# Two of sixteen state inputs made in the token layout and turned back by TensorE

## The chip, the cores and the metric

One NeuronCore of a Trainium2 chip runs the whole program in one launch. The metric is the device time of one execution in microseconds. Three runs of the kernel before gave 2841.64, 2836.22 and 2837.58 us, median 2837.58.

## What is computed

The input is 8 sequences of 1024 tokens with 256 features, all in fp32. A state space layer comes first, then a mixture of experts. Cut to what matters here:

```
xn      = layernorm(x)
u       = causal_conv4(xn @ Wx)                 # 512 channels, 4 taps
dt      = clip(sigmoid(u @ Wdt + b), 1e-4, 1)   # per token and channel
Bm, Cm  = u @ Wb, u @ Wc                        # 16 states each, per token
for each token t, channel d, state n:
    s[d,n] = exp(-dt[t,d]*A[d,n]) * s[d,n] + dt[t,d]*Bm[t,n]*u[t,d] + 1e-6
    y[t,d] = sum_n s[d,n]*Cm[t,n] + D[d]*u[t,d]
x       = x + (y * silu(z)) @ Wout
x       = x + top-2-of-8 experts(layernorm(x)) + gated shared expert(layernorm(x))
```

## The kernel before

The 8192 tokens are cut into 32 chunks of 256. Four chunks make a sequence, so the scan state is carried from the first to the second, third and fourth chunk of each sequence and starts from zero in the first. The 512 channels lie as 4 blocks (`KD`) of 128 partitions with the 256 tokens of the chunk along the free axis, so one state of one chunk is a tile of 128x1024, handled in two halves of 128x512, each in one of three PSUM banks (`V_BANKS`) that are used in turn.

`run` calls `Body.__call__` once per chunk on every engine, and each call walks 16 slots written out by hand. A call works on three chunks at once: `scan` is the chunk whose state n is scanned in slot n, `proj` is the next one (convolution, dt, B, C, z), and `post` is the one before (output projection, norm, routing, shared expert). `norm` is the one after `proj`. Each engine has its own program order, and the engines meet only at semaphores. For one state n of `scan`:

- GpSimd (POOL) multiplies `dtu` = dt*u by row n of B: `b_times_dtu`, L1036, written to one of 8 tiles `v` in `room`. It does this five slots ahead (`MUL_LEAD`). `dtu` itself is made by `dt_times_u`, L1013, just before state 0 of the next chunk, in slot 11.
- ScalarE (ACT) makes the decay factors exp(-dt*A) in `decays`, L798, three slots ahead, and adds 1e-6 while it moves the input into a PSUM bank: `add_eps`, L814, one call per half, the second half one slot ahead, the first half two slots ahead. A bank is free when the half that used it three halves earlier is scanned and used.
- VectorE (DVE) runs the scans, L1248, four of 128x256 per state. For states in `BY_POOL` the scan writes to SBUF (`room`) and POOL multiplies by C (L1025) in the next slot; ACT keeps the last column for the next chunk (`keep_last`, L819). For the other states the scan stays in PSUM, DVE multiplies by C (L1257, twice 128x512) and copies the last column (L1262).
- TensorE (PE) turns the product back to the token layout and sums over states in PSUM: `state_transpose`, L600, two slots behind.

Around these stand the steps that the change meets. In slot 11 ACT takes tanh of the second half of z (L869, into `zs`) and DVE finishes the gate in `proj_gate` (L1223, two instructions). In slot 15 DVE subtracts for the low part of the input (L1208) and makes the last third of the shared expert's hidden layer (`gated`, L1327). In slot 0 PE then transposes state 15, runs `shared_down` (L685), and starts the four convolution runs of `proj` (L552, 24 matmuls each, in slots 0, 1, 3 and 4) with post_y, skip, post_out (L616) and transposes between them. The fourth run ends in `uT` on ACT (L847) in slot 5, from which b, dt and everything behind it follow. In slots 11, 12 and 14 PE runs the shared expert's `gate_up` (L667).

SyncE (SP) writes the 32x256 rows of B and C of `proj` to DRAM and loads them back broadcast over all partitions (`load_b`, `load_c`). After the 32 chunks come 72 expert tiles of 256 rows, which have their own loop.

## Time and profile before

| | us |
|---|---|
| median of 3 runs | 2837.58 (2836.22 to 2841.64) |
| the profiled execution, its own time | 2837.99 |
| its span, first to last instruction | 2836.2 |
| outside the span | 1.8 |
| PE busy | 2515.6 (89%) |
| DVE busy | 2229.7 (79%) |
| ACT busy | 2030.7 (72%) |
| POOL busy | 2237.1 (79%) |
| mean granted TensorE clock | 0.957 of full speed |

The busy shares are over the whole span. The 32 chunks fill the first 2200 us or so and the expert tiles the rest, and the two parts have different limits, so the shares of one part must be read from a stretch inside it. A busy PE is an engine with matmuls in its pipe, not one at its peak: the same matmul takes twice as long at the lower of its two clocks (1.2 instead of 2.4 GHz).

### The profile page before, as it was taken

The numbers are of one execution on the slowest core, as the hardware profiler recorded it, in microseconds if no ns is written. First come the engines' busy times: TensorE is split into PE (matmuls) and PEld (weight loads), VectorE is DVE, ScalarE is ACT, GpSimd is POOL, SyncE is SP. The second block draws the span as 40 slices with busy tenths as digits, with TensorE's granted clock in tenths as the row PEclk, the third lists the DMA queues.
The fourth block names the chain that finished last, engine by engine and source line by source line (L and its number), as shares of the span: only waits on it lengthen the run. The fifth ranks groups of instructions, "written<-read, shape, count | busy, mean of one in ns | idle before, by whom it ended". The sixth has DMA issues, their size and how long they took to land.

```text
span 2836.2 us, 48476 instructions
## 1 busy us (share of the span) xinstructions
PE 2515.6 (89%) x15232; PEld 2200.4 (78%) x15232; DVE 2229.7 (79%) x4890; ACT 2030.7 (72%) x4675; POOL 2237.1 (79%) x1354
## 2 busy tenths in 40 slices
PE   7788888888888898988898888889887699999998
PEld 4777877777777788877787777778776488888887
DVE  2999999999999999999999999999996233333332
ACT  2888888888888888888888888888884133333332
POOL 1999999999999999999999999999994133333333
PEclk9899999999999999999999999999996899999999
DMA  4222222222222222222222322222220588888886
GB/s 177 76 82 88 79 80 87 79 80 104 88 83 82 95 79 87 87 79 80 87 80 83 105 83 83 84 94 80 87 80 15 158 199 200 202 201 202 201 200 153
DMA packets 138181, 309.62 MB, mean 109 GB/s; under 512 B 15040, under 2 KB 79680, under 8 KB 137792
## 3 DMA queue, kind: packets, MB, share of 16 engines
q1 hardware_dynamic: 110848, 270.03, 30.7%
q0 software_dynamic: 27072, 36.46, 6.5%
q8 instruction: 121, 1.98, 0.3%
q14 instruction: 140, 1.15, 0.1%
HBM read 258.42 MB, written 48.01 MB: 108 GB/s over the span
## 4 chain that ended last, share of the span: by engine, by line
PE 40%; DVE 34%; ACT 14%; issue 9%; DMA 1%; POOL 1%; DVEq 0%; SPq 0%; POOLq 0%; ACTq 0%
PE bank L667 13%; DVE bank L1248 13%; PE bank L685 9%; DVE room L1248 8%; PE bank L552 7%; DVE room L1257 6%; ACT room L798 6%; ACT bank L814 4%; PE bank L600 3%; PE bank L616 2%; PE bank L530 2%; PE bank L589 1%; PE bank L563 1%; PE bank L723 1%; ACT bank L856 1%
## 5 line engine op out<-in xcount | busy, mean ns | idle before, releaser
L1036 POOL TENSOR_TENSOR room<-dtu,b_all 128x1024 f32<-128x1024 f32 x512 | 1205.7, 2375 | 18.3 <-DVE dtu L1425 13.9
L798 ACT ACTIVATE room<-room,neg_a 128x256 f32<-128x256 f32 x2048 | 868.0, 497 | 0.8 <-DVE room L1214 0.8
L814 ACT ACTIVATE bank<-room,eps_col 128x512 f32<-128x512 f32 x1024 | 695.0, 682 | 234.7 <-DVE carry L1262 163.6
L600 PE MATMUL bank<-ident,room 128*128 128x128 f32 x4096 | 558.0, 284 | 169.3 <-POOL room L1025 85.6
L600 PEld LDWEIGHTS bank<-ident,room 128*128 128x128 f32 x4096 | 484.9, 146 | 225.6 <-POOL room L1025 95.1
L1248 DVE TENSOR_TENSOR_SCAN bank<-room,carry,bank 128x256 f32<-128x256 f32 x864 | 578.0, 734 | 20.6 <-ACT bank L814 20.1
L1025 POOL TENSOR_TENSOR room<-room,c_all 128x1024 f32<-128x1024 f32 x224 | 533.0, 2379 | 46.3 <-issue 28.8
L1162 POOL DMA_INDIRECT out<-room,ids x144 | 223.9, 1555 | 408.5 <-ACT room L996 183.7
L1327 DVE SCALAR_TENSOR_TENSOR hid<-hid,bank 128x256 f32<-128x256 f32 (+1 forms) x312 | 130.2, 417 | 420.3 <-ACT hid L909 374.5
L1248 DVE TENSOR_TENSOR_SCAN room<-room,carry,bank 128x256 f32<-128x256 f32 x672 | 448.2, 726 | 11.1 <-ACT bank L814 10.5
L552 PE MATMUL bank<-xnT,w_conv 128*128 128x256 f32 x3072 | 404.6, 288 | 7.0 <-ACT xnT L837 5.5
L667 PE MATMUL bank<-room 128*128 128x256 f32 (+1 forms) x1728 | 398.4, 380 | 2.3 <-issue 2.3
L552 PEld LDWEIGHTS bank<-xnT,w_conv 128*128 128x128 f32 x3072 | 379.7, 190 | 11.2 <-ACT xnT L837 5.8
L1257 DVE TENSOR_TENSOR room<-bank,c_all 128x512 f32<-128x512 f32 x576 | 379.7, 677 | 0.0
L667 PEld LDWEIGHTS bank<-room 128*128 128x128 f32 (+1 forms) x1728 | 308.0, 182 | 59.8 <-issue 2.6
L909 ACT ACTIVATE hid<-bank 128x256 f32<-128x256 f32 (+1 forms) x312 | 117.6, 377 | 255.5 <-PE bank L667 235.1
L667 PE MATMUL bank<-xn2T,w_gu 128*128 128x256 f32 (+1 forms) x768 | 213.1, 427 | 52.0 <-DVE base L1316 52.0
L563 PE MATMUL bank<-uT,w_dt 128*128 128x256 f32 x1024 | 231.6, 379 | 0.0
L667 PEld LDWEIGHTS bank<-xn2T,w_gu 128*128 128x128 f32 (+1 forms) x768 | 150.6, 205 | 89.4 <-DVE base L1316 59.6
L563 PEld LDWEIGHTS bank<-uT,w_dt 128*128 128x128 f32 x1024 | 189.6, 190 | 23.6 <-issue 0.4
L685 PE MATMUL bank<-room,hid 128*128 128x256 f32 (+1 forms) x864 | 198.8, 379 | 1.4 <-issue 1.4
L1248 DVE TENSOR_TENSOR_SCAN bank<-room,bank 128x256 f32<-128x256 f32 x288 | 175.7, 673 | 15.4 <-ACT bank L814 15.0
(150 smaller groups left out, 2948.3 us busy)
## 6 DMA issues: line engine op xcount, KB each, us to landing
b_all<-b_scratch SPq DMA_DIRECT2D x128, 512.0 KB, 4.0
c_all<-b_scratch SPq DMA_DIRECT2D x128, 512.0 KB, 5.2
room<-in_wgu SPq DMA_DIRECT2D x72, 704.0 KB, 5.8
room<-in_wd SPq DMA_DIRECT2D x72, 384.0 KB
room<-x_by_expert SPq DMA_DIRECT2D x72, 260.0 KB
x_in<-in_x SPq DMA_DIRECT2D x32, 256.0 KB, 6.0
x<-in_x SPq DMA_DIRECT2D x32, 256.0 KB, 2.7
out<-x SPq DMA_DIRECT2D x32, 256.0 KB, 4.3
```

Of the source, the lines that this page charges most:

```text
L552: last = mm(pr_bank[1 - half][:, j * TC:(j + 1) * TC], w_conv[w_part][:, t, b, col:col + P], xnT[x_part][:, b, t:t + TC], start=(n == 0 an ...
L563: last = mm(pr_bank[half][:, j * TC:(j + 1) * TC], w_dt[:, b, col:col + P], uT[c.par][:, b, :], start=(b == 0), stop=(b == KD - 1))
L600: last = mm(tr_bank[k][:, b * P:(b + 1) * P], v[n % VRING][:, b, k * P:(k + 1) * P], ident[:, :], is_transpose=True, start=False, stop=(n ...
L667: last = mm(bank[0:rows, g * TC:(g + 1) * TC], w[:, b, col:col + rows], xT[:, b, :], start=(b == 0), stop=(b == KM - 1))
L685: last = mm(dn_bank(tiled)[:, k * DM:(k + 1) * DM], hid[0:rows, hid_slot(c, m), k * P:(k + 1) * P], w[0:rows, m, :], start=(m == 0), stop= ...
L798: last = af(da[n % RING][:, b, :], dt[c.par][:, b, :], ACT.Exp, scale=neg_a[:, b, n:n + 1])
L814: af(v_slot(c, n, h)[:, :], v[n % VRING][:, 2 * h:2 * h + 2, :].rearrange("p b t -> p (b t)"), ACT.Identity, bias=eps_col[:, 0:1]).then_in ...
L1025: nc.gpsimd.tensor_tensor(out=s, in0=s, in1=row, op=ALU.mult).then_inc(pool_product, 1)
L1036: nc.gpsimd.tensor_tensor(out=v[n % VRING][:, :, :], in0=dtu[:, :, :], in1=row, op=ALU.mult) \
L1162: nc.gpsimd.indirect_dma_start(out=out[:, :], out_offset=bass.IndirectOffsetOnAxis(ap=ids[t.pos][:, k:k + 1], axis=0), in_=yt[t.par][:, k, ...
L1248: last = vec_e.tensor_tensor_scan(s, da[n % RING][:, b, :], p, init, ALU.mult, ALU.add)
L1257: vec_e.tensor_tensor(out=v[n % VRING][:, 2 * h:2 * h + 2, :], in0=v_slot(c, n, h)[:, :].rearrange("p (j t) -> p j t", j=2), in1=row, op=A ...
```

## The change

States 13 and 15 no longer get their input from POOL and `add_eps`. Instead PE transposes `dtu` into the token layout once per chunk (`turn_dtu`, two parts of four 128x128 transposes each), ACT copies each part from bank `pr_bank[1]` to `dtuT` (`take_dtu`), and ACT then makes `dtuT` * B + 1e-6 with B as a column per token (`b_times_turned`, two activations of 128x512 per state). PE turns the result back into the scan's two banks (`turn_state`, four transposes per half). The columns of B come from DRAM by two new DMAs of SP per chunk (`load_b_tok`). `turn_dtu` part 0 stands in slot 15, part 1 in slot 0 between state 15's transposes and `shared_down`; the convolution waits until both are copied (`dtuT_ready`), as they use its bank. `b_times_turned` stands in ACT's slots 11 and 13, `turn_state` in PE's slots 11 to 14.

State 1 joins `BY_POOL`: its product with C moves from DVE to POOL, and its last column from DVE to ACT. `dt_times_u` moves from slot 11 to slot 10. The shared expert's hidden tiles become three instead of a ring of six, so its first tanh waits for the previous chunk's `shared_down`; the expert tiles get their hidden layer in `room`.

```diff
-BY_POOL = [0, 2, 4, 6, 8, 10, 12]
+BY_POOL = [0, 1, 2, 4, 6, 8, 10, 12]
+TURNED = [13, 15]
...
+        dtuT = sb("dtuT", [P, NT, DI])
+        b_tok = [sb(f"b_tok{i}", [P, NT, len(TURNED)]) for i in range(2)]
...
-        hid = sb("hid", [P, THRING, TC])
+        hid = sb("hid", [P, HB, TC])
...
+            def load_b_tok(c):
...
+                sp_wait(b_written, c.index * 16 + 16)
...
+                sp_wait(tok_ready, inputs(c.plus(-1), 0)[1])
+                for k in range(NT):
+                    src = b_scratch[c.par, TURNED[0]:NS:2, k * P:(k + 1) * P].rearrange("n t -> t n")
+                    sp.dma_start(b_tok[c.par][:, k, :], src, allow_slow_non_contiguous=True)                       .then_inc(b_tok_loaded, 16)
...
                 if half == 0 and j == 0:
+                    wait(pe, dtuT_ready, c.index * NT)
                     wait(pe, h_ready, units_out(c.plus(-3), 1))
...
+            def turn_dtu(c, k, post):
+                pe.wait_ge(dtu_ready, c.index + 1)
+                pe.wait_ge(zs_done, (c.index + 1) * NT)
+                if post:
+                    pe.wait_ge(h_ready, units_out(post, 1))
+                wait(pe, dtuT_ready, c.index * NT + k)
+                transposes(pr_bank[1], [dtu[:, b, k * P:(k + 1) * P] for b in range(KD)]).then_inc(dtu_turned, 1)
...
+            def turn_state(c, n, h):
+                pe.wait_ge(tok_ready, inputs(c, n + 1)[1])
+                bank_free(*before(c, n, h))
+                for j in range(2):
+                    for k in range(NT):
+                        b = 2 * h + j
+                        last = nc.tensor.transpose(v_slot(c, n, h)[:, j * TC + k * P:j * TC + (k + 1) * P],
+                                                   v_tok[n % VRING][:, k, b * P:(b + 1) * P], ident[:, :])
+                last.then_inc(turn_ready, 1)
...
                     for slot in range(NS):
+                        if scan and slot == 12:
+                            turn_state(scan, 13, 1)
...
+                        if slot == 0 and scan and post:
+                            turn_dtu(scan, 1, late_of(post))
...
+                        if scan and slot + 2 in TURNED:
+                            turn_state(scan, slot + 2, 0)
+                        if proj and slot == 15:
+                            turn_dtu(proj, 0, post)
                         if post:
                             for u in units_of(slot, GU_SLOT):
                                 gate_up(post, u, w_gu, xn2T, False)
+                        if scan and slot == 14:
+                            turn_state(scan, 15, 1)
...
+            def take_dtu(c, k):
+                act.wait_ge(dtu_turned, c.index * NT + k + 1)
+                af(dtuT[:, k, :], pr_bank[1][:, :], ACT.Copy).then_inc(dtuT_ready, 1)
+
+            def b_times_turned(c, n):
+                act.wait_ge(dtuT_ready, c.index * NT + NT)
+                act.wait_ge(b_tok_loaded, (c.index + 1) * NT * 16)
+                act.wait_ge(tr_ready, c.index * NS + n - VRING + 1)
+                i = turned_inputs(n)
+                for k in range(NT):
+                    af(v_tok[n % VRING][:, k, :], dtuT[:, k, :], ACT.Identity, scale=b_tok[c.par][:, k, i:i + 1],
+                       bias=eps_col[:, 0:1]).then_inc(tok_ready, 1)
...
                         c, n = ahead(slot + 1)
-                        if c:
+                        if c and n not in TURNED:
                             add_eps(c, n, 1)
+                        if scan and slot + 2 in TURNED:
+                            b_times_turned(scan, slot + 2)
+                        if scan and post and slot == 0:
+                            take_dtu(scan, 1)
...
+                        if proj and slot == 15:
+                            take_dtu(proj, 0)
...
+                        if scan and proj and slot == 10:
+                            dt_times_u(proj)
                         n = slot + MUL_LEAD
-                        if scan and n < NS:
+                        if scan and n < NS and n not in TURNED:
                             b_times_dtu(scan, n)
```

Two places of the order are shown. On ACT, the start of slot 11 (line numbers differ between the two programs: L798/L871 `decays`, L814/L887 `add_eps`, L869/L955 the tanh into `zs`), before:

```order
L798 ACTIVATE room<-room,neg_a 128x256 x3
L814 ACTIVATE bank<-room,eps_col 128x512 [waits dve_kept,v_mul]
L869 ACTIVATE zs<-bank 128x512 [waits y_ready,pr_ready]
L897 ACTIVATE xn_1<-token_f 128x2 [waits token_done]
L899 ACTIVATE token_f<-token_f,chunk_col 128x2 [waits id_ready]
L814 ACTIVATE bank<-room,eps_col 128x512 [waits dve_kept,v_mul]
```

and now:

```order
L871 ACTIVATE room<-room,neg_a 128x256 x3
L887 ACTIVATE bank<-room,eps_col 128x512 [waits dve_kept,v_mul]
L900 ACTIVATE room<-dtuT,eps_col,b_tok 128x512 [waits tr_ready,b_tok_loaded,dtuT_ready]
L900 ACTIVATE room<-dtuT,eps_col,b_tok 128x512
L955 ACTIVATE zs<-bank 128x512 [waits y_ready,pr_ready]
L983 ACTIVATE xn_1<-token_f 128x2 [waits token_done]
L985 ACTIVATE token_f<-token_f,chunk_col 128x2 [waits id_ready]
```

The two new activations stand between the last input of state 12 and the tanh of z; the input of state 13 behind it is gone.

On ACT, the end of slot 15 and slot 0, now (L995 is the tanh of the shared expert's last third, L892 is `take_dtu`):

```order
L995 ACTIVATE hid<-bank 96x256 [waits dn_ready,gu_ready]
L887 ACTIVATE bank<-room,eps_col 128x512 [waits dve_kept,v_mul]
L892 ACTIVATE dtuT<-bank 128x512 [waits dtu_turned]
L871 ACTIVATE room<-room,neg_a 128x256 [waits half_ready]
L871 ACTIVATE room<-room,neg_a 128x256 x3
L887 ACTIVATE bank<-room,eps_col 128x512 [waits half_ready,v_mul]
L892 ACTIVATE dtuT<-bank 128x512 [waits dtu_turned]
```

Before, the same rows stand there without the two of L892.

On PE, the end of slot 15 and slot 0, now (L635 `state_transpose`, L564 dtu `turn_dtu`, L746 `shared_down`, L587 the convolution):

```order
L635 MATMUL bank<-ident,room 128x128 x7
L564 MATMUL bank<-ident,dtu 128x128 [waits h_ready,dtuT_ready,zs_done,dtu_ready]
L564 MATMUL bank<-ident,dtu 128x128 x3
L746 MATMUL bank<-w_dn,hid 128x256 [waits mix_done,h_ready,xn_low]
L746 MATMUL bank<-w_dn,hid 128x256 x5
L587 MATMUL bank<-xnT,w_conv 128x256 [waits dtuT_ready,h_ready,zs_done,evac]
L587 MATMUL bank<-xnT,w_conv 128x256 x15
```

Before, the transposes of state 15 (L600) are followed directly by `shared_down` (L685), and the convolution (L552) has no wait on `dtuT_ready`.

## Rows read from the trace of the kernel before

**Rows 1.** Stretch: busy us of PE, PEld, DVE, ACT, POOL; clock, DMA share, GB/s
```profile
1380.00:1660.00 280.00, 246.84 (x1648) 221.18 (x1649) 269.60 (x571) 243.57 (x562) 267.51 (x157) 0.97 0.27 87
```

**Rows 2.** Waits of DVE, 400 to 2200 us: us, times, longest
```profile
DVE bank L1248 <- ACT bank L814: 28.7, 44, 0.9
DVE room L1248 <- ACT bank L814: 13.4, 26, 0.7
```

**Rows 3.** POOL timeline, first and last of 25: start, us, line
```profile
376.67 2.37 POOL L1013 TENSOR_TENSOR dtu<-room,uT 128x1024 f32<-128x1024 f32 x1
...
1954.96 2.38 POOL L1013 TENSOR_TENSOR dtu<-room,uT 128x1024 f32<-128x1024 f32 x1
```

**Rows 4.** Group on POOL, 400 to 2200 us: busy us, mean ns
```profile
L1036 POOL TENSOR_TENSOR room<-dtu,b_all 128x1024 f32<-128x1024 f32 x427 | 1005.6, 2375 | 3.9 <-PE bank L600 0.5
```

**Rows 5.** DVE timeline, slot 11 of a second chunk
```profile
1493.08 0.67 DVE L1257 TENSOR_TENSOR room<-bank,c_all 128x512 f32<-128x512 f32 x1
...
1494.40 0.16 DVE L1307 RECIPROCAL w_sh<-r_den 128x2 f32<-128x2 f32 x1
...
1494.90 1.28 DVE L1223 SCALAR_TENSOR_TENSOR zs<-zs,bank 128x512 f32<-128x512 f32 x2
```

**Rows 6.** ACT timeline, the same slot
```profile
1493.91 0.69 ACT L814 ACTIVATE bank<-room,eps_col 128x512 f32<-128x512 f32 x1 [0.18 <-DVE carry L1262]
1494.54 0.58 ACT L869 ACTIVATE zs<-bank 128x512 f32<-128x512 f32 x1
1495.02 0.20 ACT L897 ACTIVATE xn<-token_f 128x2 uint32<-128x2 f32 x1
```

**Rows 7.** ACT and DVE timelines, slot 11 of a first chunk
```profile
1429.58 0.58 ACT L869 ACTIVATE zs<-bank 128x512 f32<-128x512 f32 x1
...
1429.63 1.28 DVE L1223 SCALAR_TENSOR_TENSOR zs<-zs,bank 128x512 f32<-128x512 f32 x2
```

**Rows 8.** Groups on ACT, 400 to 2200 us
```profile
L814 ACT ACTIVATE bank<-room,eps_col 128x512 f32<-128x512 f32 x859 | 583.2, 682 | 202.8 <-DVE carry L1262 140.9 <-DVE room L1257 52.8 <-DVE room L1248 5.2
L847 ACT ACTIVATE uT<-bank,vec 128x256 f32<-128x256 f32 x104 | 42.9, 463 | 8.5 <-PE bank L552 8.2
...
L823 ACT ACTIVATE xn<-x,o_shift,o_rstd 128x256 f32<-128x256 f32 x56 | 30.6, 593 | 12.5 <-POOL o_shift L1050 7.5 <-ACT b_row L861 5.1
```

**Rows 9.** DVE, PE, ACT, end of slot 15 to uT, second chunk
```profile
1445.65 0.68 DVE L1208 TENSOR_TENSOR xnT<-bank,xnT 128x512 fp32r<-128x512 f32 x1
1447.20 2.83 PE L685 MATMUL bank<-w_dn,hid 128*128 128x256 f32 x12 [0.39 <-issue]
1449.69 3.20 PE L552 MATMUL bank<-xnT,w_conv 128*128 128x256 f32 x24
...
1471.42 0.82 ACT L847 ACTIVATE uT<-bank,vec 128x256 f32<-128x256 f32 x2
```

**Rows 10.** ACT in slot 0 of the same chunk
```profile
1446.67 1.70 ACT L798 ACTIVATE room<-room,neg_a 128x256 f32<-128x256 f32 x4
1448.49 0.69 ACT L814 ACTIVATE bank<-room,eps_col 128x512 f32<-128x512 f32 x1
```

**Rows 11.** The same stretch of a third and a first chunk
```profile
1249.33 0.68 DVE L1208 TENSOR_TENSOR xnT<-bank,xnT 128x512 fp32r<-128x512 f32 x1
...
1255.05 3.20 PE L552 MATMUL bank<-xnT,w_conv 128*128 128x256 f32 x24
...
1275.62 0.84 ACT L847 ACTIVATE uT<-bank,vec 128x256 f32<-128x256 f32 x2 [0.46 <-PE bank L552]
...
1381.36 0.68 DVE L1208 TENSOR_TENSOR xnT<-bank,xnT 128x512 fp32r<-128x512 f32 x1
...
1406.81 0.84 ACT L847 ACTIVATE uT<-bank,vec 128x256 f32<-128x256 f32 x2 [0.80 <-PE bank L552]
```

**Rows 12.** Stretches around a slow start: length, PE busy, clock, DMA
```profile
1049.50:1053.00 3.50, 0.05 (x1) 1.00 0.00 0
1053.00:1055.00 2.00, 1.87 (x9) 0.59 0.64 149
```

More of the change, by code:

```diff
@@ L90, in dve_products, with turned_inputs, pool_inputs @@
     return n - pool_products(n)
+def turned_inputs(n):
+    return sum(1 for m in TURNED if m < n)
+def pool_inputs(n):
+    return n - turned_inputs(n)
 def units_of(slot, slots):
@@ L907, in gate @@
                 act.wait_ge(gu_ready, c.index * UNITS + u + 1)
-                act.wait_ge(dn_ready, c.index + HEAD)
-                af(hid[0:rows, hid_slot(c, u), :], bank[0:rows, 0:TC], ACT.Tanh, scale=0.5).then_inc(th_ready, 1)
+                act.wait_ge(dn_ready, c.index + HEAD + (0 if tiled else 1))
+                af(hid_tile(c, u, tiled)[0:rows, :], bank[0:rows, 0:TC], ACT.Tanh, scale=0.5).then_inc(th_ready, 1)
             class Body(Phases):
@@ L939, in start @@
                     decays(Chunk(0, 0), 2)
+                    for k in range(NT):
+                        take_dtu(Chunk(0, 0), k)
                     take_normed(Chunk(0, 1))
```

50 lines of the change are left out of this document (37 added, 13 removed).

## The prediction

> **What bounds the kernel now.** I read the busy time by stretches first. In a stretch of 280 us inside the chunks DVE is busy for 269.6 us, POOL for 267.5, PE for 246.8 and ACT for 243.6 [rows 1]. So two engines are nearly full, and the shares alone do not say which of them sets the pace. The waits do. Nearly all that DVE waits for in 1800 us is ACT filling its banks, 28.7 + 13.4 us in 70 waits [rows 2], and the same list names POOL nowhere. POOL is full, but it works five slots ahead, and nobody stands waiting for a B product. The period of a chunk comes from the starts of dt*u on POOL: (1954.96 - 376.67) / 24 = 65.76 us [rows 3].
>
> Within a chunk I follow the chain of work through the timelines. Let T be the moment when DVE has finished state 15's product, seen as the start of its next instruction, L1208. From T to uT in slot 5 two paths run side by side. DVE goes through states 0 to 5 and lets ACT get to uT at 1471.42, that is T + 25.77 in a second chunk [rows 9]. PE goes through transposes, shared_down and four convolution runs; its first run starts at 1449.69, T + 4.04, and in that chunk it is done before ACT is. In a third chunk PE starts its runs only at 1255.05, T + 5.72, and ACT waits 0.46 us for it and starts uT at T + 26.29; in a first chunk, where the scans are shorter, ACT waits 0.80 us and starts at T + 25.45 [rows 11]. The mean of the three is 25.84. So over this third of the chunk DVE and PE are within a microsecond of each other. Behind uT comes a piece in which ACT sets the pace, and from slot 10 to T it is DVE, instruction behind instruction.
>
> **DVE gives away state 1's product.** In the trace the two products and two copies of one state take 1494.40 - 1493.08 = 1.32 us [rows 5] (it is state 11's, the same instructions). They leave slot 1, which is in the T to uT part, so DVE's path becomes 25.77 - 1.32 = 24.45 us. The scan itself costs DVE the same.
>
> **PE's path gets a new condition.** The first convolution run must wait until ACT has copied both parts of dtu. ACT's slot 0 has the decays at 1446.67 and the input of state 1 at 1448.49, 0.69 us long, ended at 1449.18 [rows 10]. In front of the decays comes one copy, whose pitch I take from the tanh of the same size and the same kinds of memory, 1495.02 - 1494.54 = 0.48 us [rows 6]; of it 0.12 us fall into the wait that now stands before 1448.49. Behind comes the second copy, 0.58 us [rows 6]. That is 1449.18 + 0.36 + 0.58 = 1450.12, T + 4.5, and with a handover of 0.1 us the run starts at T + 4.6 instead of T + 4.04. PE's own part, the four transposes of part 1, is hidden: shared_down waits 0.39 us for DVE's last gated product anyway [rows 9]. From the start of the runs to uT it is 1275.62 - 1255.05 = 20.6 us where ACT waited for PE [rows 11]. With no other wait of PE uT so starts at T + 25.1 to 25.2; the warm chunk's run was 0.2 us quicker, so I take T + 25.0. Against 25.84 now the gain is 0.84 us per chunk, not 1.32: PE is now the last to arrive.
>
> The bounds of this term. Below, uT cannot come before DVE's path, T + 24.45, a gain of 1.39. Above, if PE starts with its clock low: in the stretch of 2 us behind T its granted clock was 0.59, after 3.5 us in which it was busy for 0.05 us [rows 12]; the run then starts at T + 5.72 as in rows 11, plus about 0.5 for the transposes, and uT at T + 26.8, a loss of 1.0. I take the warm value because the change fills just this idle time: PE now has turn_state of state 15 and turn_dtu of part 0 in front of T, and state 14's transposes move behind them. The Trainium skill speaks against that (TensorE: Matmul & The Clock Gate, Part 4: PE-mode transpose): transposes do not count as busy for the clock, and all the work that is added is transposes. By that rule the clock would be low behind T in every chunk, and the total would be that of the second rival below.
>
> **ACT gets two activations in front of the tanh of z.** This is the term that costs. In slot 11 ACT does the second half of state 12's input (released by DVE, the row says, after 0.18 us of waiting), then the tanh of z at 1494.54, ended at 1495.12. DVE's gate needs it: the first gate instruction starts at 1494.90, and two take 1.28 us, so the second starts at 1495.50 or so [rows 5, 6]. The slack is 0.38 us. In a first chunk the tanh ends at 1430.16 and the second gate instruction starts about 1430.23, a slack of 0.07 [rows 7]. Now two activations of 128x512 with a scale column and a bias column stand ahead of the tanh. Such an activation of 128x256 has a mean of 593 ns, one with bias alone 463 ns for 256 columns and 682 ns for 512 [rows 8]. So the size adds 0.22 us, and I get 0.81 us from start to end. Started one behind the other they overlap by about 0.1 us (0.58 long, 0.48 apart [rows 6]), so the pitch is about 0.72. Two shift the tanh by 1.44 us, and DVE stands still for 1.44 - 0.38 = 1.06 us, or 1.37 us in a first chunk: (3 x 1.06 + 1.37) / 4 = 1.14 us per chunk. The lower bound is the pitch of a plain copy, 0.48, which gives 0.66; the upper one no overlap, 0.81, which gives 1.32. Behind this place DVE works without a gap up to T, so the stall goes into the period whole.
>
> **What I cost at nothing.** POOL loses two B products and gains one C product, at 2.375 us each [rows 4] a relief of 2.4 us per chunk; as nobody waits for POOL, it is slack. State 1's product on POOL must be there when PE turns state 1 in slot 3. PE comes there behind two runs of 3.2 us [rows 9] and the skip term, so not before T + 4.6 + 6.4 = T + 11, and POOL has three products of 2.4 us to make from the end of scan 0, about T + 4, on: T + 11.2. That is close, and if POOL were late, PE's runs would be late with it. PE's turn_state is covered by PE's idle time in slots 11 to 14; if that cover is gone, it is the second half of scan 13, behind gate_up, that waits. The two DMAs of SP stand ahead of the loads of B for the next chunk, which are five slots ahead of their use; DVE's list of waits has no DMA in it [rows 2]. If they took some ten us in the queue, POOL would be late in slot 11. The inputs that ACT no longer makes (four per chunk) and the four turned ones are about even. The expert tiles do not change.
>
> **The sum.** +1.14 - 0.84 = +0.30 us per chunk, times 31 chunks with a next one = +9.3. At the end the last chunk has no gate and no convolution and keeps the whole 1.32 us; at the start the two parts of dtu are turned and copied in series, about +1.0. Together +9 us on the profiled execution's 2838.0 (0.4 above the median), so **2847 us**.
>
> **Rivals.** First, faster: the copies land early enough for PE's run to start on time, and the turned activations are short. The place is uT in slot 5 at T + 24.45, the price 24.45 - 25.77 = -1.32, and with the stall at its lower bound +0.66 the chunk is 0.66 us shorter, 2838 - 20 = 2818 us. It decides from the point where the gate's stall is below what DVE's path gives back. For it: ACT waits for DVE in much of slot 0 to 5 (140.9 us of its waits are on the carry copies [rows 8]); against it: the slack of 0.07 to 0.38 us at the gate is plain in the rows.
>
> Second, much slower: the clock stays low behind T (the rule above). Then uT is at T + 26.8, and with the stall +1.0 + 1.14 = +2.1 us per chunk, 2903 us. For it: the stretch at 0.59. Against it: PE's idle time ahead of T falls from 3.5 us to about 1.
>
> Third, no change: gain and stall cancel, or neither is there because the parts that I take as serial have slack, 2838 us, within the 0.2% (5.7 us) that a measurement can tell from nothing.
>
> **Chances.** My forecast 0.44, its own range 2840 to 2862; the faster rival 0.26; the low clock 0.11; no change 0.19. The range for 8 in 10 is 2808 to 2880: it takes in the faster rival at 2818, and leaves out the full price of the low clock and the outer part of the faster one, as with a gain of 1.3 us and no stall. Faster by over 0.2% 0.27, within 0.2% 0.22, slower 0.51.
>
> **What would show it.** In the new profile the second gate instruction on DVE (the zs group) should have a wait on ACT's zs of about 1 us per chunk; if that wait is absent, the costly term is wrong. The first uT of slot 5 should be preceded by a wait of ACT for the convolution in nearly every chunk, 0.3 to 0.6 us; if instead DVE or the bank fills end last there, PE is not the new bound. The PE run should start at T + 4.6, with a granted clock of 1.00 behind T. The turned activations should have a mean near 0.8 us. A wait of DVE's scan on PE in states 13 or 15, or any wait on the columns of B, would be a cost that I left out.

## The result and the profile after

Four runs of the changed kernel gave a median of 2892.18 us (2891.4 to 2893.08), beside 2837.89 us for the kernel before (2836.22 to 2841.64, four runs in the same comparison): a ratio of 1.019, with a 95% interval from 1.0172 to 1.0207. The change costs 54 us. I had predicted 2847 and a range of 2808 to 2880, so the sign was right and the size was not, and the time lies outside the range. The profiled execution took 2893.08 us, its span is 2891.1 us.

The starts of dt*u on POOL, 24 chunks apart as in [rows 3]:

```profile
382.33 2.41 POOL L1108 TENSOR_TENSOR dtu<-room,uT 128x1024 f32<-128x1024 f32 x1
...
2002.33 2.41 POOL L1108 TENSOR_TENSOR dtu<-room,uT 128x1024 f32<-128x1024 f32 x1
```

The period is (2002.33 - 382.33) / 24 = 67.50 us instead of 65.76. That is 1.74 us per chunk, and 31 chunks of it are 54 us, so the loss is in the chunks.

The stretch of 280 us that answers to [rows 1]:

```profile
1380.00:1660.00 280.00, 251.71 (x1699) 225.50 (x1697) 257.32 (x535) 244.03 (x563) 250.60 (x149) 0.98 0.27 83
```

DVE is busy for 257.3 us instead of 269.6, POOL for 250.6 instead of 267.5. Both engines were relieved, and the kernel is slower. No engine is full now, so the time has gone into waits between them. The list of waits from 400 to 2200 us (engine, line, releaser: us, times, longest) names them. In the changed program L1347 is the scan, L1319 the gate, L1378 the residual addition, L887 `add_eps`, L900 `b_times_turned`, L955 the tanh of z, L933 uT, L661 `turn_state`, L677 post_out:

```profile
PE bank L661 <- ACT room L900: 121.0, 51, 3.5
...
DVE bank L1347 <- ACT bank L887: 38.4, 61, 0.9
...
DVE x L1378 <- PE bank L677: 31.6, 24, 1.5
...
DVE zs L1319 <- ACT zs L955: 27.6, 26, 1.3
...
ACT uT L933 <- PE bank L587: 16.8, 26, 0.8
...
PE bank L564 <- ACT dtuT L892: 15.6, 27, 0.6
```

Two of these I had forecast (the gate's, and uT's on the convolution), two I had not: DVE now waits 31.6 us for the output projection (7.8 us before), and PE waits in `turn_dtu`. The wait of `turn_state` is the longest of the list, but it is PE's own: no engine waits for `turn_state` (L661) anywhere in the full list.

**The gate.** Slot 11 of a first chunk, ACT and DVE:

```profile
1465.81 1.50 ACT L900 ACTIVATE room<-dtuT,eps_col,b_tok 128x512 f32<-128x512 f32 x2
1465.85 0.68 DVE L1319 SCALAR_TENSOR_TENSOR zs<-zs,bank 128x512 f32<-128x512 f32 x1
1467.22 0.57 ACT L955 ACTIVATE zs<-bank 128x512 f32<-128x512 f32 x1
1467.82 0.69 DVE L1319 SCALAR_TENSOR_TENSOR zs<-zs,bank 128x512 f32<-128x512 f32 x1 [1.29 <-ACT zs L955]
```

The two turned activations stand ahead of the tanh, and the second gate instruction waits 1.29 us for it, where in [rows 7] the pair ran in one piece. Over 26 chunks the waits are 27.6 us, 1.06 us each.

**The start of a chunk.** Here T is 1350.27, a third chunk like the one of [rows 11]. L635 transposes states, L564 transposes dtu, L746 is `shared_down`, L587 the convolution, L728 `gate_up`:

```profile
1343.99 1.89 PE L728 MATMUL bank<-xn2T,w_gu 128*96 128x256 f32 x8
...
1347.46 1.04 PE L635 MATMUL bank<-ident,room 128*128 128x128 f32 x8
...
1350.27 0.69 DVE L1304 TENSOR_TENSOR xnT<-bank,xnT 128x512 fp32r<-128x512 f32 x1
1350.35 1.09 PE L635 MATMUL bank<-ident,room 128*128 128x128 f32 x8 [1.85 <-DVE room L1356]
1351.29 0.58 ACT L892 ACTIVATE dtuT<-bank 128x512 f32<-128x512 f32 x1
1352.02 1.08 PE L564 MATMUL bank<-ident,dtu 128*128 128x128 f32 x4 [0.58 <-ACT dtuT L892]
1352.89 3.98 PE L746 MATMUL bank<-w_dn,hid 128*128 128x256 f32 x12
1356.53 3.20 PE L587 MATMUL bank<-xnT,w_conv 128*128 128x256 f32 x24
...
1377.05 0.84 ACT L933 ACTIVATE uT<-bank,vec 128x256 f32<-128x256 f32 x2 [0.63 <-PE bank L587]
```

And the stretches of it (length, then busy us of PE, PEld, DVE, ACT and POOL; granted clock, DMA share, GB/s):

```profile
1350.00:1352.00 2.00, 1.09 (x8) 0.87 (x9) 1.97 (x6) 2.00 (x5) 2.00 (x1) 0.99 0.39 118
1351.50:1352.00 0.50, 0.00 (x0) 0.01 (x1) 0.50 (x2) 0.50 (x2) 0.50 (x1) 0.95 0.81 205
1352.00:1354.00 2.00, 1.98 (x7) 1.82 (x8) 2.00 (x4) 2.00 (x6) 2.00 (x2) 0.50 0.99 277
```

Between `gate_up`, which ends at 1345.88, and `shared_down` PE has nothing but transposes, with a gap of 1.85 us and one of 0.58 us in which part 1 of `turn_dtu` waits until ACT has copied part 0 out of the same bank. The granted clock is still 0.95 in the half microsecond of this second gap and 0.50, the lower level of 1.2 GHz, right behind it. `shared_down` takes 3.98 us where it took 2.83 [rows 9], and the convolution starts at T + 6.26 instead of T + 4.6. Of the 24 chunks from 400 to 1980 us, 19 start it later than T + 5.5, all of them with a slow `shared_down` (3.88 to 4.42 us); in the other five it takes 2.76 us.

Before the change 5 of 24 chunks started the convolution later than T + 5.5. That count hides that the clock fell there too: `shared_down` took over 3 us in 15 of 24 chunks, as in the third chunk of [rows 11]:

```profile
1250.89 4.52 PE L685 MATMUL bank<-w_dn,hid 128*128 128x256 f32 x12 [0.39 <-issue]
```

It began about T + 1.6 to T + 1.9 then and begins at T + 2.2 to T + 2.6 now. So the low clock is not new. More chunks meet it, 19 instead of 15, and the convolution starts at T + 6.2 to T + 6.4 in them, where it had started at T + 4.8 to T + 5.7.

I cut every chunk at uT of slot 5 as the prediction did. Each number is a mean over these chunks, in us, read off the timelines; the row predicted sets the forecast's T + 4.6 against the mean before:

| | T to convolution | T to uT | uT to next T | period |
|---|---|---|---|---|
| before | 4.80 | 25.80 | 39.95 | 65.75 |
| after | 5.95 | 26.48 | 41.02 | 67.50 |
| difference | +1.15 | +0.68 | +1.07 | +1.75 |
| predicted | -0.2 | -0.84 | +1.14 | +0.30 |

### The profile page after: what moved, and what is told of

It reads as the page before. It is cut to its first block, busy times and chain, and to the rows that moved or that the text cites. A ratio compares the mean times of both kernels' runs of the same rounds, so it can differ in the third digit from the quotient of the medians.

```text
span 2891.1 us, 50358 instructions
## 1 busy us (share of the span) xinstructions
PE 2581.9 (89%) x16000; PEld 2267.0 (78%) x16000; DVE 2199.6 (76%) x4778; ACT 2068.0 (72%) x4763; POOL 2166.2 (75%) x1322
## 3 DMA queue, kind: packets, MB, share of 16 engines
q14 instruction: 140, 1.15, 0.1%
## 4 chain that ended last, share of the span: by engine, by line
PE 46%; ACT 24%; DVE 19%; issue 8%; DMA 2%; POOL 1%; SPq 0%; DVEq 0%; ACTq 0%; POOLq 0%
PE bank L728 13%; PE bank L587 10%; PE bank L746 10%; DVE bank L1347 8%; ACT room L871 8%; ACT bank L887 7%; DVE room L1347 5%; DVE room L1356 4%; PE bank L564 3%; PE bank L677 3%; PE bank L635 3%; ACT room L900 2%; PE bank L624 1%; ACT bank L942 1%; PE bank L784 1%
## 5 line engine op out<-in xcount | busy, mean ns | idle before, releaser
L1129 POOL TENSOR_TENSOR room<-dtu,b_all 128x1024 f32<-128x1024 f32 x448 | 1058.0, 2376 | 24.0 <-DVE dtu L1524 13.9
L871 ACT ACTIVATE room<-room,neg_a 128x256 f32<-128x256 f32 x2048 | 869.4, 500 | 0.8 <-DVE room L1310 0.8
L1120 POOL TENSOR_TENSOR room<-room,c_all 128x1024 f32<-128x1024 f32 x256 | 608.8, 2378 | 154.8 <-issue 81.0
L887 ACT ACTIVATE bank<-room,eps_col 128x512 f32<-128x512 f32 x896 | 607.9, 684 | 157.2 <-DVE carry L1361 107.1
L635 PE MATMUL bank<-ident,room 128*128 128x128 f32 x4096 | 537.7, 276 | 61.0 <-DVE room L1356 53.6
L635 PEld LDWEIGHTS bank<-ident,room 128*128 128x128 f32 x4096 | 468.0, 142 | 98.7 <-DVE room L1356 61.2
L1347 DVE TENSOR_TENSOR_SCAN bank<-room,carry,bank 128x256 f32<-128x256 f32 x768 | 517.7, 735 | 33.3 <-ACT bank L887 30.3
L1347 DVE TENSOR_TENSOR_SCAN room<-room,carry,bank 128x256 f32<-128x256 f32 x768 | 513.9, 726 | 14.0 <-ACT bank L887 11.4
L587 PE MATMUL bank<-xnT,w_conv 128*128 128x256 f32 x3072 | 405.6, 288 | 4.7 <-ACT dtuT L892 2.2
L1426 DVE SCALAR_TENSOR_TENSOR room<-room,bank 128x256 f32<-128x256 f32 (+1 forms) x216 | 90.8, 420 | 413.8 <-ACT room L995 369.3
L728 PE MATMUL bank<-room 128*128 128x256 f32 (+1 forms) x1728 | 398.0, 380 | 2.5 <-issue 2.5
L587 PEld LDWEIGHTS bank<-xnT,w_conv 128*128 128x128 f32 x3072 | 380.8, 191 | 9.2 <-issue 2.4
L728 PEld LDWEIGHTS bank<-room 128*128 128x128 f32 (+1 forms) x1728 | 307.9, 182 | 60.2 <-issue 2.9
L995 ACT ACTIVATE room<-bank 128x256 f32<-128x256 f32 (+1 forms) x216 | 82.5, 382 | 247.3 <-PE bank L728 232.4
L661 PE MATMUL bank<-ident,room 128*128 128x128 f32 x512 | 85.8, 293 | 154.4 <-ACT room L900 148.2
L661 PEld LDWEIGHTS bank<-ident,room 128*128 128x128 f32 x512 | 61.3, 149 | 184.7 <-ACT room L900 163.1
L746 PE MATMUL bank<-room 128*128 128x256 f32 (+1 forms) x864 | 198.7, 379 | 1.4 <-issue 1.4
L728 PE MATMUL bank<-xn2T,w_gu 128*128 128x256 f32 (+1 forms) x768 | 196.4, 403 | 0.4 <-DVE base L1415 0.4
```

The lines of the kernel that those rows point to most:

```text
L587: last = mm(pr_bank[1 - half][:, j * TC:(j + 1) * TC], w_conv[w_part][:, t, b, col:col + P], xnT[x_part][:, b, t:t + TC], start=(n == 0 an ...
L635: last = mm(tr_bank[k][:, b * P:(b + 1) * P], v[n % VRING][:, b, k * P:(k + 1) * P], ident[:, :], is_transpose=True, start=False, stop=(n ...
L728: last = mm(bank[0:rows, g * TC:(g + 1) * TC], w[:, b, col:col + rows], xT[:, b, :], start=(b == 0), stop=(b == KM - 1))
L746: last = mm(dn_bank(tiled)[:, k * DM:(k + 1) * DM], hid_tile(c, m, tiled)[0:rows, k * P:(k + 1) * P], w[0:rows, m, :], start=(m == 0), sto ...
L871: last = af(da[n % RING][:, b, :], dt[c.par][:, b, :], ACT.Exp, scale=neg_a[:, b, n:n + 1])
L887: af(v_slot(c, n, h)[:, :], v[n % VRING][:, 2 * h:2 * h + 2, :].rearrange("p b t -> p (b t)"), ACT.Identity, bias=eps_col[:, 0:1]).then_in ...
```

## The experiments

Theory A, formed on this profile: the 54 us are the gate stall (about 1.07 us per chunk) and the low clock with `turn_dtu`'s wait behind T (what separates 26.48 from 25.0), and state 1's move brings nothing. The rivals say that a stall taken away only uncovers the next one, or that the clock is not the cause. Each run was compared with the kernel before on the same chip, whose median was 2839.8 to 2841.2 us there.

### 1. Turned activations behind the tanh

```diff
-                        if scan and slot + 2 in TURNED:
-                            b_times_turned(scan, slot + 2)
...
                         if proj:
                             project(proj, slot)
+                        if scan and slot + 2 in TURNED:
+                            b_times_turned(scan, slot + 2)
```

> The two turned activations of a state are moved behind the tanh of z (slot 11) and the projection step of slot 13. Theory A (the gate's stall is serial): DVE's wait on ACT's zs, 0.97 to 1.29 us per chunk in the changed kernel, goes to nothing and the chunk is shorter by that, 31 x 1.05 = 33 us: 2859 us. Rival B (the stall hides a wait that stands behind it, on TensorE's turned banks or its gate_up): the zs wait goes, but DVE waits for the bank of state 13 or for hid instead, and the time stays above 2880 us.

Measured: 2880.25 us (2876.86 to 2882.61), 12 us less than the change, ratio to the kernel before 1.0143 [1.0125, 1.0161]. The wait at the gate is gone, but uT to T takes 41.18 us, as long as with the stall. What took its place stands in a first chunk's slots 11 and 12:

```profile
1458.97 1.11 PE L661 MATMUL bank<-ident,room 128*128 128x128 f32 x4 [3.34 <-ACT room L900]
1459.87 3.62 PE L728 MATMUL bank<-xn2T,w_gu 128*128 128x256 f32 x8
1463.29 1.06 PE L661 MATMUL bank<-ident,room 128*128 128x128 f32 x4
1464.38 1.27 DVE L1347 TENSOR_TENSOR_SCAN bank<-room,bank 128x256 f32<-128x256 f32 x2 [2.63 <-PE bank L661]
```

```profile
1461.00:1463.00 2.00, 2.00 (x6) 1.55 (x6) 0.75 (x2) 0.03 (x1) 0.66 (x1) 0.50 0.17 63
```

PE stands for 3.34 us at the first half of `turn_state`. Behind that its clock is at 0.50, `gate_up` takes 3.62 us where the row of 1343.99 above has 1.89 for the same count, and the second half of `turn_state` stands behind it in PE's queue. DVE's scan of state 13 waits 2.63 us. The 12 us that were won came at the other end, where only 9 of 24 chunks started the convolution late. So rival B holds for this placement: the gate stall went, and another wait of the same size took its place.

### 2. Real matmuls between the last transposes

Three matmuls of 128x256 that add zero to a bank in use stand between the transposes of states 14 and 15. PE carries them as six.

```diff
+            def stay_warm(n):
+                for _ in range(n):
+                    mm(tr_bank[0][:, 0:TC], zeros[:, 0, 0:P], w_gu[:, 0, 0:TC], start=False, stop=False,
+                       skip_group_check=True)
...
                             state_transpose(post, NS - 2)
+                            stay_warm(3)
                             state_transpose(post, NS - 1)
```

> Three real matmuls of 256 columns that add zero are put on TensorE between the transposes of states 14 and 15, in time in which it now waits for DVE. Theory A (the clock falls since TensorE does nothing but transposes between gate_up of slot 14 and shared_down): the clock stays at 1.00 behind T, the first convolution run starts at T + 4.7 in all chunks instead of T + 6.3 in three of four, 24 x 1.6 = 38 us less: 2854 us. Rival B (the clock falls from the idle time or the phase alone, or the three matmuls only add work): the start stays at T + 6.3 and the time within 0.2% of 2892 us or above.

Measured: 2856.54 us (2854.99 to 2859.33), ratio 1.0055 [1.0037, 1.0073], 36 us less than the change. A third chunk with T = 1330.41:

```profile
1328.48 1.46 PE L641 MATMUL bank<-w_gu,zeros 128*128 128x256 f32 x6
1330.48 1.09 PE L635 MATMUL bank<-ident,room 128*128 128x128 f32 x8 [0.55 <-issue]
1332.15 0.63 PE L564 MATMUL bank<-ident,dtu 128*128 128x128 f32 x4 [0.58 <-ACT dtuT L898]
1332.62 2.76 PE L751 MATMUL bank<-w_dn,hid 128*128 128x256 f32 x12
```

```profile
1333.00:1335.00 2.00, 2.00 (x10) 1.73 (x10) 2.00 (x5) 2.00 (x5) 2.00 (x2) 1.00 0.97 336
```

The wait of 0.58 us is still there and the clock stays at 1.00. The convolution starts at T + 4.6 in every chunk, the value that the prediction had worked out, and uT at T + 25.16. Work was added to PE, and the kernel became 36 us faster: the clock is worth that. Whether it takes real matmuls, or whether any work in that idle time would do, this run can't tell: it changes both, and no run put more transposes there.

### 3. Part 0 of dtu copied early

```diff
                         if c:
                             decays(c, n)
+                        if proj and slot == 15:
+                            take_dtu(proj, 0)
...
-                        if proj and slot == 15:
-                            take_dtu(proj, 0)
```

> ScalarE takes part 0 of the transposed dt u right behind the decays of slot 15, where it waits for DVE, and not at the end of the slot. Theory A (TensorE's 0.58 us wait on dtuT and the 0.48 us copy are on the path to the first convolution run): the wait goes, the run starts 0.5 us earlier in every chunk, 31 x 0.5 = 16 us: 2876 us; more if the shorter wait keeps the clock up in some chunks. Rival B (the clock decides, the wait is hidden in its low stretch): within 5 us of 2892.

Measured: 2841.96 us (2841.01 to 2847.7, ten runs), ratio 1.001 [1.0001, 1.002]. I had expected 2876; it took away 50 us. The start of a first chunk with T = 1386.53:

```profile
1386.67 1.09 PE L635 MATMUL bank<-ident,room 128*128 128x128 f32 x8 [1.57 <-DVE room L1356]
1387.60 0.60 PE L564 MATMUL bank<-ident,dtu 128*128 128x128 f32 x4
1388.11 2.83 PE L746 MATMUL bank<-w_dn,hid 128*128 128x256 f32 x12
1390.73 2.49 PE L587 MATMUL bank<-xnT,w_conv 128*128 128x256 f32 x19
```

```profile
1388.00:1390.00 2.00, 2.00 (x11) 1.71 (x10) 2.00 (x5) 2.00 (x6) 2.00 (x2) 1.00 0.96 256
```

Without the wait `shared_down` starts at T + 1.6 and takes 2.83 us in every chunk: none of 24 is late, the convolution starts at T + 4.31 and uT at T + 24.72 on average. The transposes of the change are all still there. My expectation priced the wait alone and named what the clock might add without pricing it; that was the larger part. The period is 65.77 us, the same as before the change, made of -1.08 at the front and +1.09 at the gate.

### 4. State 1 back on VectorE

```diff
-BY_POOL = [0, 1, 2, 4, 6, 8, 10, 12]
+BY_POOL = [0, 2, 4, 6, 8, 10, 12]
```

> State 1's product goes back to DVE, the turned inputs stay. Theory A (TensorE arrives last at uT of slot 5, with ScalarE waiting 0.56 to 0.84 us for it): giving DVE its 1.32 us back costs only what goes beyond the slack, at most 1.32 - 1.1 = 0.2 us in most chunks: 2892 to 2900 us. Rival B (DVE's path still counts): 1.3 us per chunk, 2933 us.

Measured: 2893.42 us (2891.1 to 2893.98), ratio 1.0184 [1.0165, 1.0202], the same as the change. That is two effects which cancel, and not one that is absent. In the 12 of 24 chunks in which PE is late, uT starts at T + 26.7 to T + 26.9 as in the change, and DVE's 1.32 us are hidden. In the other 12 PE is on time, seven chunks more than in the change, and in ten of these it is DVE that arrives last, at T + 25.78 instead of T + 25.2. One of them, with T = 474.03:

```profile
499.81 0.82 ACT L933 ACTIVATE uT<-bank,vec 128x256 f32<-128x256 f32 x2
```

Why the clock stays up in more chunks here is not shown. Experiment 10 asks again with PE on time.

### 5. State 1's move alone, in the kernel before

The same line of `BY_POOL` gets its 1 in the kernel before.

> The kernel before, with state 1's C product on GpSimd and nothing else. DVE is relieved of 1.32 us per chunk; GpSimd, which is busy 62.8 of 65.8 us per chunk before, gets 2.4 us more and now has nothing of states 13 and 15 taken off. Theory A (GpSimd becomes the bound, and state 1's move was worth nothing to begin with, as the fourth experiment says): 2838 to 2860, with DVE or ACT waiting for GpSimd's input products. Rival (DVE sets the path and its 1.32 us are real in every chunk): 2838 - 1.32 x 26 = 2804, up to 2815.

Measured: 2861.68 us (2860.68 to 2864.07), ratio 1.0078 [1.0063, 1.0094], slower by 21 us. PE waits for POOL's products; before, the same wait came to 65.9 us in 28 times:

```profile
PE bank L600 <- POOL room L1025: 180.5, 80, 5.1
...
ACT x_in L823 <- POOL p_shift L1050: 65.4, 25, 3.7
```

T to uT went up to 26.62 us. So POOL cannot take this product for nothing while it makes the inputs of states 13 and 15 as well, and the relief that the prediction costed at nothing is what lets state 1's move pay.

### 6. The first three together

> The first three experiments together: turned activations behind tanh z, three zero-adding matmuls between the last two state transposes, early copy of dt u. Theory A (the first experiment's waits of DVE for turn_state are the price of its late activations, and stay): 2842 less the 12 us that the first experiment won = 2830, from 2824 to 2836, with DVE waiting for turn_state in state 13. Rival: those 12 us were partly won at the clock (one chunk in two of the first experiment had its convolution at T+4.6 instead of T+6.3), and with the clock already up nothing is left: 2840 to 2850.

Measured: 2854.7 us (2854.57 to 2855.59), ratio 1.0052 [1.0037, 1.0068]. Both expectations are too low. The convolution starts at T + 4.31 in every chunk, but uT to T takes 41.54 us. Experiment 12 takes the added matmuls out again.

### 7. State 13's turned activations in slot 9

With the early copy, and:

```diff
-                        if scan and slot + 2 in TURNED:
-                            b_times_turned(scan, slot + 2)
+                        if scan and slot in (9, 13):
+                            b_times_turned(scan, 13 if slot == 9 else 15)
```

> The change with the copy of dt u right behind slot 15's decays (the third experiment, 2842), and also with state 13's two turned activations issued in slot 9 instead of 11, so that they no longer stand ahead of tanh z. State 15's stay in slot 13. Theory A (the gate stall is real time in every chunk and needs nothing else): the wait of the second gate instruction for ACT's tanh z (0.97 to 1.29 us, mean 1.07) is gone, 1.07 x 26 = 28 us, so 2814, from 2806 to 2822, faster than the kernel before. Theory B (whoever is relieved of one wait meets the next, as in the first experiment, which won 12 of 28): the stall goes, but the 1.5 us of ACT in slot 9 pushes its copies and tanh of gate_up, and the time is 2828 to 2842. Above 2842 both are wrong.

Measured: 2839.39 us (2837.64 to 2840.78, eleven runs), ratio 0.9999 [0.999, 1.0008]; 2.6 us less than experiment 3. Theory A's 28 us did not come, and B's range holds it. In the same place of the same chunk the tanh starts at 1435.32 in experiment 3, and here at:

```profile
1435.37 0.57 ACT L955 ACTIVATE zs<-bank 128x512 f32<-128x512 f32 x1
```

The activations left slot 11, and the tanh did not move. In both timelines ACT works from uT (1411.15 and 1411.19) to this tanh with no gap but one of 0.17 us, so work that is added anywhere in between moves its end by its own length. In the chunks that are not the first of a sequence the tanh does come 0.2 to 0.3 us sooner here; in some of them experiment 3 has a second gap of 0.17 us ahead of `add_eps`, which is filled here. DVE's wait at the gate is 0.78 us instead of 1.06:

```profile
DVE zs L1319 <- ACT zs L955: 20.3, 26, 1.0
```

The stall is for the most part the length of ACT's queue from uT to the gate.

### 8. Real matmuls in the kernel before

The edit of experiment 2 in the kernel before.

> The kernel before with the same three zero-adding matmuls between the last two state transposes, nothing else. In it T to the first convolution matmul is 4.04 us where the clock stays up and up to 5.72 where not, and T to uT 25.4 to 26.3. Theory A (the drop of the clock behind T cost the kernel before something too, and the path runs by uT): T to the convolution 4.6 in all chunks, T to uT 25.2, so 0.3 to 1.1 us less per chunk, mean 0.6 x 26 = 16 us: 2822, from 2814 to 2830. Rival (the added matmuls cost as much as they bring, the path in the kernel before is DVE's in those chunks): 2835 to 2845.

Measured: 2835.36 us (2831.15 to 2838.39, eleven runs), ratio 0.9983 [0.9974, 0.9992]. That lies at the edge of the rival's range and below the kernel before by 5 us. The added matmuls did help the clock: `shared_down` takes over 3 us in 8 of 24 chunks instead of 15. Behind T it brings nothing on average (T to uT is 25.90 us), since in most of the others uT starts at T + 25.77, where DVE's path ends, and six of 24 chunks still start late, two of them at T + 6.5, later than any before. In one of them, T = 1051.31:

```profile
1051.38 1.09 PE L600 MATMUL bank<-ident,room 128*128 128x128 f32 x8 [2.29 <-DVE room L1263]
1052.87 5.46 PE L690 MATMUL bank<-w_dn,hid 128*128 128x256 f32 x12 [0.39 <-issue]
```

```profile
1053.00:1055.00 2.00, 2.00 (x5) 1.65 (x6) 2.00 (x4) 1.72 (x4) 2.00 (x2) 0.50 0.96 197
```

Here PE stood idle for 2.29 us between the added matmuls and the transposes of state 15, and the clock fell all the same. The period in this profile is 65.85 us against 65.75 before, so the 5 us are not seen in the chunks from 400 to 1980 us; where they come from stays open.

### 9. The tanh first, then the turned activations, then the decays

With the early copy, and in ACT's slot 11 alone:

```diff
+                        if proj and slot == 11:
+                            project(proj, slot)
                         c, n = ahead(slot + DECAY_LEAD)
-                        if c:
+                        if c and slot != 11:
                             decays(c, n)
...
                             b_times_turned(scan, slot + 2)
+                        c, n = ahead(slot + DECAY_LEAD)
+                        if c and slot == 11:
+                            decays(c, n)
...
-                        if proj:
+                        if proj and slot != 11:
                             project(proj, slot)
```

> The early copy of dt u (the third experiment, 2842), and in ScalarE's slot 11 this order: tanh z first, then add_eps of state 12, the two turned activations of state 13, and only then the decays of state 14, whose scan comes three slots later. The trace of the early turn (seventh experiment) has ScalarE without a gap from uT at T+24.7 to tanh z, 23 us later: what is put anywhere ahead of tanh z pushes it. Here the turned activations and 1.7 us of decays come behind it, and the activations still end a microsecond sooner than in the third experiment, so turn_state is not late as in the first. Theory A (ScalarE's queue ahead of tanh z is what sets uT to T'): no wait of DVE for zs, none worth a microsecond for turn_state, uT to T' back at 38.8 to 40.4 us, 1.07 x 26 = 28 us less than 2842: 2814, from 2806 to 2822, and faster than the kernel before. Rival (the microsecond comes back at the next thing that ScalarE feeds, banks or decays of state 14): 2830 to 2842.

Measured: 2824.22 us (2816.85 to 2831.38, six runs), ratio to the kernel before 0.9939 [0.9923, 0.9956]. This beats both kernels, by 17 us and by 68 us. Slot 11 of a first chunk:

```profile
1421.98 0.60 ACT L955 ACTIVATE zs<-bank 128x512 f32<-128x512 f32 x1
1423.18 0.69 ACT L887 ACTIVATE bank<-room,eps_col 128x512 f32<-128x512 f32 x1 [0.60 <-DVE carry L1366]
1423.81 1.50 ACT L900 ACTIVATE room<-dtuT,eps_col,b_tok 128x512 f32<-128x512 f32 x2
1424.17 1.27 DVE L1324 SCALAR_TENSOR_TENSOR zs<-zs,bank 128x512 f32<-128x512 f32 x2
1425.22 1.69 ACT L871 ACTIVATE room<-room,neg_a 128x256 f32<-128x256 f32 x4
1425.36 1.12 PE L661 MATMUL bank<-ident,room 128*128 128x128 f32 x4 [2.55 <-ACT room L900]
1426.27 2.88 PE L728 MATMUL bank<-xn2T,w_gu 128*128 128x256 f32 x8
1429.62 1.27 DVE L1352 TENSOR_TENSOR_SCAN bank<-room,bank 128x256 f32<-128x256 f32 x2 [0.68 <-PE bank L661]
```

The tanh is done 1.6 us before DVE's pair begins, and the pair runs in one piece. The decays of state 14, 1.69 us that nobody needs for three slots, stand last. uT to T is 40.41 us instead of 41.04, a gain of 0.63 rather than 1.07. The measured time lies between the two ranges that were expected. The rest went to what ACT feeds next, though not to the banks or decays that the rival named: `gate_up` still runs at the low clock behind PE's 2.55 us of waiting, and DVE waits 0.68 us for the second half of `turn_state`.

### 10. The ninth, with state 1 back on VectorE

> The same as the ninth, and state 1's C product back on VectorE. Theory A (DVE's work in the slots before T+24.7 lies beside the path by uT, as in the fourth experiment, and beside ScalarE's queue behind it): within 4 us of the ninth. Rival (with the two late steps gone DVE is the path again, and its 1.32 us per chunk count): 20 to 34 us above the ninth.

The edit of experiment 4 on top of the ninth. Measured: 2845.91 us (2841.74 to 2850.08, ten runs), ratio 1.0017 [1.0008, 1.0026], 21.7 us above the ninth. The rival holds. T is 1447.42 in the chunk of this row, and uT starts at T + 25.77 with no wait for PE:

```profile
1473.19 0.82 ACT L933 ACTIVATE uT<-bank,vec 128x256 f32<-128x256 f32 x2
```

In the ninth it is T + 24.74, with a wait of 0.24 us for the convolution. So 25.77 is DVE's path with state 1's product in it, the number that the prediction had read in [rows 9]. Over 24 chunks T to uT is 25.46 us instead of 24.73, so 0.73 us of the 1.32 count, times 31 chunks 23 us; in the first chunk of a sequence uT comes at T + 24.6 either way. In experiment 4 PE was later than DVE in half of the chunks, and a better clock made up for the rest.

### 11. The new order, with the copy left late

The edit of the ninth, without the early copy.

> The change with the new order of slot 11 alone, the copy of dt u as late as the change has it, and so the low clock behind T in three chunks of four. Theory A (the two terms, clock with the copy's wait, and gate stall, add up): 2892 less 28 = 2864, T to the convolution still 6.3 us in most chunks, from 2856 to 2872. Rival (they overlap): 2875 to 2892.

Measured: 2848.15 us (2843.51 to 2854.91, ten runs), ratio 1.0026 [1.0016, 1.0035], 44 us less than the change where 28 were expected. uT to T is 40.37 us, as in the ninth. The other gain is at the front: only 6 of 24 chunks start the convolution late, instead of 19, though nothing was edited there and PE's wait of 0.58 us stands in all of them. The two terms are not independent. Reordering slot 11 also keeps PE's clock up behind T in most chunks; through which step, no run here tells.

### 12. The early copy with the first experiment's order

> The early copy of dt u (third experiment) with the turned activations behind tanh z (first), and without the added matmuls of the sixth, which came to 2855. It differs from the ninth (2824) only in where state 14's decays stand in slot 11: here ahead of tanh z and of the turned activations, there behind both. Theory A (the place of the 1.7 us of decays decides: the turned activations end 1.7 us later than in the ninth, and turn_state, gate_up behind it and DVE's scan of state 13 wait for them): 2842 to 2856, with DVE waiting for turn_state as in the first experiment (34.7 us in 24 chunks). Rival (the added matmuls made the sixth slow, and the order alone is enough): 2820 to 2832.

Measured: 2856.17 us (2853.9 to 2861.74), ratio 1.0064 [1.0047, 1.0081], as the sixth and 32 us above the ninth. T to uT is 24.72 us as in the ninth, uT to T 41.43 instead of 40.41: 1.02 x 31 = 32 us. DVE's longest line of waits is the one that replaced the gate stall in experiment 1:

```profile
DVE bank L1347 <- PE bank L661: 40.2, 25, 2.6
```

So the added matmuls did not make the sixth slow, and the order of slot 11 is worth 32 us. The expectation says that the decays' place is the only difference from the ninth. It is not quite: the ninth also has the tanh ahead of `add_eps` of state 12. The turned activations stand behind both of these in either order, and only the decays come ahead of them here and behind them there, which is why I put the 32 us down to the 1.7 us of decays. No run moved the decays alone.

## Why the prediction failed

**The gate stall** was right in place and size: 1.06 us per wait against 1.14, with the turned activations at 0.798 us each against 0.81. Its group in the changed trace:

```profile
L900 ACT ACTIVATE room<-dtuT,eps_col,b_tok 128x512 f32<-128x512 f32 x104 | 78.2, 798 | 0.0
```

What it took too narrowly is where the stall comes from, the two rows ahead of the tanh. Experiment 7 shows that most of it stays when these rows stand elsewhere in ACT's queue behind uT. The prediction had said that ACT sets the pace in that piece, and did not use it.

**DVE's path** was right with state 1's product in it: uT comes at T + 25.77 (experiment 10). Without it PE is last at T + 24.7 (experiments 3 and 9), as the prediction said; no run shows the T + 24.45 of DVE itself, because PE is later in all of them.

**PE's path** is the step that failed. The text said "I take the warm value because the change fills just this idle time", and it called the four transposes of part 1 hidden. Measured, T to uT moved by +0.68 us instead of -0.84, a miss of 1.5 us per chunk, 47 us in all, which is the whole error of 45. The warm value itself was right: where the clock stayed up, the convolution started at T + 4.6 to T + 4.7 and uT at T + 25.1 to T + 25.2 (five chunks of the change, and all of experiment 2). That is the 25.1 to 25.2 of the sum; the 0.2 us that the prediction then took off has no row behind it. What was wrong is how often it holds, in 5 chunks of 24.

**The wait of part 1 on part 0** was the term left out. I looked at the convolution's new condition and the place of ACT's copies in slot 0. But the four transposes of part 1 use the bank that ACT has yet to empty, and that copy stands last in ACT's slot 15, behind an input of 0.69 us. PE waits 0.58 us, `shared_down` begins at T + 2.2 or later instead of T + 1.6, and in the chunk shown the clock falls in that gap. Experiment 3 removed the wait alone: the clock stayed up in all 24 chunks, uT came at T + 24.72, and 50 us came back. The idle time ahead of T was misjudged besides, at about 1 us, where 1.35 to 1.85 us were left.

**Transposes and the clock.** The Trainium skill (TensorE: Matmul & The Clock Gate, Part 4: PE-mode transpose) says that transposes do not count as busy in the way matmuls do. The traces agree as far as this: in 19 of 24 chunks the clock fell in a stretch of transposes alone, and six records of real matmuls in their midst held it at 1.00 (experiment 2). They also show two limits: in experiment 3 there were only transposes in the same place and it stayed up in every chunk, more often than before the change, and in experiment 8 the added matmuls did not always hold it. By that rule I had named the second rival, T + 26.8 and 2903 us, with a chance of 0.11. Its T + 26.8 came true in 19 chunks of 24 (26.72 to 26.91), and the time lies between it and the forecast, nearer to it. But it gave the transposes as the cause, and experiment 3 shows that they alone do not bring the clock down. The wait is not enough alone either: it stands in every chunk of experiments 1, 4 and 11, with 9, 12 and 6 of 24 late. What decides between a late chunk and one on time stays open.

**What was costed at nothing.** POOL's relief was wrongly put at nothing: without it state 1's move costs 21 us (experiment 5). `turn_state` I called covered by idle time; it is so in the change, where the gate stall holds DVE back, and it is the next wait as soon as the stall goes (experiments 1 and 12). The DMAs of the B columns do not appear in the list of waits, as forecast. The smaller ring of the hidden tiles and the earlier dt*u were not tested by themselves; ACT's tanh of the hidden layer waits 8.0 us for PE in the changed kernel and 8.2 before, and dt*u on POOL 6.6 us for DVE. DVE's 31.6 us at the residual addition, which I had not forecast, shrink with the late convolution: in experiments 3 and 9 the same line has 10 us.

## What to carry to other kernels

Price a new operation by what it does to the queue behind it, up to the next engine that waits: here one copy placed three instructions too late cost 50 us, and the order of slot 11, most likely its 1.7 us of decays, 32 us. Where an engine works without a gap, its end moves by what is added, wherever that stands. When the clock already falls in some chunks of the trace, count those chunks, and price each new wait ahead of real matmuls at the low clock as well as by its length. Transposes in an idle stretch gave no certain answer either way: the same ones stood there with 19 chunks of 24 late and with none. A measurement of "worth nothing" can be two effects that cancel; ask again once something else is mended, as state 1 went from 0 to 22 us.

## What was not expected of the hardware

A wait of 0.58 us in a row of transposes tipped the clock of the real work behind them: with it `shared_down` took 3.98 us at 0.50 in the chunk shown, without it 2.83 us at 1.00 (experiment 3). Late chunks were 19, 9, 12 and 6 of 24 in the four runs that have the wait and no added matmuls (the change and experiments 1, 4 and 11), and none of 24 in experiments 3 and 9, whose PE has the same transposes in the same order. In the kernel before with added matmuls the clock fell behind a gap of 2.29 us, although real matmuls had run right ahead of it, and `shared_down` took 5.46 us.

It also fell in slot 11, where PE waits for the turned activations: `gate_up` x8 took 3.62 us in experiment 1 and 2.88 in the ninth, against 1.89 at the higher level. A slow `gate_up` is not a loss by itself. Its groups of eight take over 2.2 us in 16 of 73 cases from 400 to 2040 us in the kernel before, in 4 of 71 in the change, and in 17 of 74 in the ninth, the fastest of all. It costs time where another engine waits behind it, as DVE does for the second half of `turn_state`.
